# First router of a two-layer block: codes by the eight-maximum, positions by two products, weights worked out in the expert loop

## What is computed

```
logits = where(old_to_new == -1, -inf, x @ gate.T)      # 128 experts, 48 kept
probs  = softmax(logits); top_v, top_i = top_k(probs, 8)
top_v  = top_v / sum(top_v)
flat_e = old_to_new[top_i].reshape(-1)                  # in order of token, then rank
pos    = number of earlier entries of flat_e that are the same expert
valid  = pos < 96                                       # capacity
xb[flat_e, pos] = x[token]                              # kept ones only
out    = (silu(xb @ gate_e) * (xb @ up_e)) @ down_e     # per expert, 96 rows
final[token] += out[flat_e, pos] * top_v * valid
```

## Time and profile before

| | us |
|---|---|
| median of 3 runs (lowest, highest) | 1669.9 (1666.23, 1676.31) |
| profiled execution, its own time | 1677.43 |
| its span | 1675.6 |
| PE busy | 1406.2 (84%) |
| DVE busy | 1156.0 (69%) |
| ACT busy | 822.9 (49%) |
| POOL busy | 782.8 (47%) |
| routing phase | from about 260 to 338.7 |
| expert phase's loop | from 338.7 to 430.6 |

### The profile page before, as it was taken

One profiled execution on the slowest core, in us unless ns is written; L12 is line 12 of the kernel. 1 busy time (PEld: TensorE's weight loads), 2 busy tenths in 40 slices (PEclk: granted clock), 3 DMA queues, 4 the chain that ended last, 5 costly groups with the idle time before them and its releaser, 6 DMA issues. The chain is left out here.

```text
span 1675.6 us, 38381 instructions
## 1 busy us (share of the span) xinstructions
PE 1406.2 (84%) x14345; PEld 999.1 (60%) x14345; DVE 1156.0 (69%) x2350; ACT 822.9 (49%) x2163; POOL 782.8 (47%) x1118
## 2 busy tenths in 40 slices
PE   5988994189545899999999999999999999976675
PEld 2543342066422567777777677777777777765465
DVE  6887126923475788888888788888887888833623
ACT  3334871043132466665665565665665666632122
POOL 5100000177213366467567467566566566543443
PEclk9999996589877999999999899999999999987788
DMA  8200005066723464565565464654555555331884
GB/s 280 74 2 2 2 1 157 1 199 211 256 58 66 114 148 122 149 177 125 160 156 131 128 160 122 162 153 144 139 157 148 119 160 148 99 107 57 241 253 130
DMA packets 249433, 218.72 MB, mean 131 GB/s; under 512 B 88770, under 2 KB 224962, under 8 KB 247200
## 3 DMA queue, kind: packets, MB, share of 16 engines
q1 hardware_dynamic: 234992, 192.41, 42.7%
q0 software_dynamic: 5712, 15.60, 2.8%
q10 hardware_dynamic: 8544, 8.26, 1.6%
HBM read 133.85 MB, written 82.25 MB: 129 GB/s over the span
## 5 line engine op out<-in xcount | busy, mean ns | idle before, releaser
L1825 DVE SCALAR_TENSOR_TENSOR d_conv<-d_big,all_cw,d_conv 128x1023 f32<-128x1023 f32 (+2 forms) x192 | 245.4, 1278 | 45.6 <-ACT d_conv L2067 43.6
L1547 PE MATMUL d_big<-all_xn_t,all_w 128*128 128x512 f32 x512 | 252.6, 624 | 18.7 <-DVE d_conv L1825 11.9
L1547 PEld LDWEIGHTS d_big<-all_xn_t,all_w 128*128 128x128 f32 x512 | 93.8, 198 | 101.4 <-issue 88.2
L2166 ACT COPY d_ys<-d_big 128x128 f32<-128x128 f32 x256 | 61.0, 266 | 177.7 <-PE d_big L1715 139.8
L2301 POOL TENSOR_TENSOR d_y<-d_y,all_xn 128x256 f32<-128x256 f32 x128 | 96.9, 757 | 107.3 <-DVE d_y L1977 89.5
L1753 PE MATMUL d_big<-all_wo,d_yt 128*128 128x256 f32 x512 | 125.5, 391 | 13.8 <-DVE d_yt L1902 13.8
L2258 POOL TENSOR_TENSOR d_vs<-d_vs,d_sv 128x1024 f32<-128x1024 f32 x32 | 61.2, 1912 | 135.6 <-DMA d_vs<-turned_v_scratch 134.3
L1686 PE MATMUL d_big<-all_w,all_xn_t 128*128 128x256 f32 x512 | 122.6, 383 | 0.0
L1753 PEld LDWEIGHTS d_big<-all_wo,d_yt 128*128 128x128 f32 x512 | 96.9, 197 | 26.3 <-issue 14.4
L1876 DVE SCALAR_TENSOR_TENSOR d_AI<-d_big,d_b_col,d_decay 128x256 f32<-128x256 f32 x256 | 104.3, 474 | 2.0 <-PE d_big L1560 1.2
L1686 PEld LDWEIGHTS d_big<-all_w,all_xn_t 128*128 128x128 f32 x512 | 93.7, 190 | 17.7 <-issue 7.2
(11 more groups left out here) (436 smaller groups left out, 3483.2 us busy)
## 6 DMA issues: line engine op xcount, KB each, us to landing
turned_kq_scratch<-d_turned SPq DMA_DIRECT2D x32, 512.0 KB, 3.8
d_kq_tok<-turned_kq_scratch SPq DMA_DIRECT2D x128, 128.0 KB, 3.1
turned_v_scratch<-d_vs SPq DMA_DIRECT2D x16, 1024.0 KB, 4.1
d_vs<-turned_v_scratch SPq DMA_DIRECT2D x64, 256.0 KB, 5.6
grouped_y_scratch<-d_yx SPq DMA_DIRECT2D x32, 512.0 KB, 3.7
d_yx<-grouped_y_scratch SPq DMA_DIRECT2D x128, 128.0 KB, 3.1
all_w<-in_L_attn_W_qkvz SPq DMA_DIRECT2D x16, 768.0 KB
l_hold<-in_L_ffn_gate_up_proj SPq DMA_DIRECT2D x48, 192.0 KB, 3.5
```

The costliest lines, as they stand in the source:

```text
L1547: mm = pe.matmul(big[0][:, c, :], w_sb[par][:, k, n * DK:(n + 1) * DK], xn_t[:, k, c * 512:(c + 1) * 512], start=(k == 0), stop=(k == KD - 1))
L1825: dve.scalar_tensor_tensor(conv[:, sh:T], src[:, 0:T - sh], cw[:, bass.ds(g, 1), COLUMN_OF[j], 3 - sh], conv[:, sh:T], ALU.mult, ALU.add). ...
```

## The change

The gate and map loads are issued in attention, behind the clearing of the second mixture's slots (`clear_slots`). Logits are shifted four tiles at a time. `chosen` is made by ScalarE. Positions come out of two products: `ahead_t = sum of chosen of earlier tiles with ones + chosen with before`, then times `same`, in fp32. The code of each chosen expert (`fine`) plus its position stands at the expert's place, all else far below it (a code is at least 2^14), and an eight-maximum takes the eight codes, in the order of codes, not of probabilities. Doubles are found by one 8x8 comparison per token. The 128-wide one-hots are 64 compares with a pointer scalar; the rank product moves from POOL to VectorE, the row product from VectorE to ScalarE.

Since codes are no longer in rank order, the weights need the index search and the 64 picks after all; these, a second slot calculation and the matching of slots with weights run on VectorE in the expert loop (`weigh(e)`), and ScalarE's diagonals stand at experts 41, 43, 45 and 47.

```diff
+class Routing:
+    def load(self, sp, gate_t, old_to_new):
+        sp.dma_start(self.gate[:, :, :], gate_t.rearrange("(k p) e -> p k e", p=P)).then_inc(self.loaded, 16)
...
 # router0_phase, TensorE
-            for t in range(TT):
-                pe.wait_ge(chosen_s, t + 1)
-                pe.transpose(tr_ps[:, t, :], chosen[:, t, :], ident_bf[:, :]).then_inc(turned_s, 1)
...
+            def ahead_of(t):
+                pe.wait_ge(chosen_s, t + 1)
+                for b in range(t):
+                    pe.matmul(at_ps[t // 4][:, t % 4, :], chosen[:, b, :], ones[:, :], start=(b == 0), stop=False,
+                              skip_group_check=True)
+                pe.matmul(at_ps[t // 4][:, t % 4, :], chosen[:, t, :], before[:, :], start=(t == 0), stop=True,
+                          skip_group_check=True).then_inc(at_mm, 1)
+            def position(half):
+                pe.wait_ge(at_c, half + 1)
+                for t in range(4 * half, 4 * half + 4):
+                    pe.matmul(ps_ps[half][:, t % 4, :], ahead_t[:, t, :], same[:, :], start=True, stop=True,
+                              skip_group_check=True).then_inc(pos_mm, 1)
...
+            for t in range(6):
+                ahead_of(t)
+            position(0)
+            for t in range(6, TT):
+                ahead_of(t)
+            position(1)
 # ScalarE
+            def choose(t):
+                act.wait_ge(taken_s, t + 1)
+                act.activation(chosen[:, t, :], taken[:, t, :], ACT.Relu, scale=-1.0).then_inc(chosen_s, 1)
+            def keep_ahead(half):
+                act.wait_ge(at_mm, 4 * half + 4)
+                act.copy(ahead_t[:, 4 * half:4 * half + 4, :], at_ps[half][:, :, :]).then_inc(at_c, 1)
...
+                act.activation(hot_id[:, t, :, 0, :], hot_e[:, t, :, :], ACT.Copy, scale=row_f[:, 0:1]).then_inc(low_s, 1)
 # VectorE
+            def best(t):
+                dve.wait_ge(exp_s, t + 1)
+                dve.max(top[:, t, :], prob[:, t, :]).then_inc(top_s, 1)
+                if t:
+                    keep_code(t - 1)
+                dve.wait_ge(top_s, t + 1)
+                dve.match_replace(taken[:, t, :], top[:, t, :], prob[:, t, :], -1.0).then_inc(taken_s, 1)
+            def sorted_codes(half):
...
+                dve.tensor_tensor(code[:, at, :], ps_ps[half][:, :, :], fine[:, at, :], ALU.add).then_inc(code_s, 1)
+                dve.wait_ge(code_s, half + 1)
+                for t in range(4 * half, 4 * half + 4):
+                    dve.max(top_code[:, t, :], code[:, t, :]).then_inc(top_code_s, 1)
+            shift_logits(0)
+            best(0)
+            best(1)
+            shift_logits(1)
...
-                for r in range(TOPK):
-                    dve.scalar_tensor_tensor(junk[:, t * TOPK + r, :], iota_f[:, :], idx_f[:, t, r:r + 1], packed[:, t, :],
-                                             ALU.is_equal, ALU.mult, accum_out=code[:, t, r:r + 1]).then_inc(code_s, 1)
...
-                dve.tensor_tensor(hot_c[:, t, :, :], iota_b[:, :].unsqueeze(1).broadcast_to([P, TOPK, P]),
-                                  row_b[:, t, :].unsqueeze(2).broadcast_to([P, TOPK, P]), ALU.is_equal).then_inc(hot_s, 1)
+                for r in range(TOPK):
+                    dve.tensor_scalar(hot_c[:, t, r, :], iota_b[:, :], row_v[:, t, r:r + 1], None, ALU.is_equal).then_inc(hot_c_s, 1)
 # experts0_phase, VectorE, after product(e) of each expert
+            def weigh(e):
+                if e < TT:
+                    index_of(e)
+                elif e == TT:
+                    dve.wait_ge(idx_s, TT)
+                    then(dve.tensor_copy(idx_f[:, :, :], top_idx[:, :, :]))
+                elif e <= LAST_CODE:
+                    for k in range(CODES * (e - FIRST_CODE), min(CODES * (e - FIRST_CODE) + CODES, NR)):
+                        code_of(k)
...                                      # LAST_CODE = 30; then split, doubles, place, shares, weights_by_slot: one an expert
 # ScalarE
-                if e % 4 == 0 and e < 2 * TT:
-                    diagonals(e // 4)
+                if e >= EK - TT and e % 2:
+                    diagonals((e - EK + TT) // 2)
```

More of the change, by code:

```diff
@@ L629, in router0_phase @@
+def router0_phase(nc, xn, xn_t, routing, ranks, xn_dram, buffers, gu_t, down_t):
     with ExitStack() as ctx:
@@ L808, in _ @@
-            then(dve.tensor_copy(idx_f[:, :, :], top_idx[:, :, :]))
-            for t in range(TT):
-                dve.wait_ge(count_mm, 4 * (t // 4) + 4)
-                then(dve.tensor_copy(count[:, t, :], ct_ps[t // 4][:, t % 4, :]))
-                if t == 0:
-                    dve.tensor_copy(total[:, 0, :], count[:, 0, :]).then_inc(total_s, 1)
-                else:
-                    dve.wait_ge(total_s, t)
-                    dve.tensor_tensor(total[:, t, :], total[:, t - 1, :], count[:, t, :], ALU.add).then_inc(total_s, 1)
@@ L835, in _ @@
-            n += 2
-            dve.wait_ge(v, n)
-            for r in range(1, TOPK):
-                then(dve.tensor_tensor(equal[:, :, 0:r], new_f[:, :, 0:r], new_f[:, :, r:r + 1].broadcast_to([P, TT, r]),
-                                       ALU.is_equal))
-                then(dve.tensor_reduce(extra[:, :], equal[:, :, 0:r], AX.X, ALU.add))
-                then(dve.tensor_tensor(pos_f[:, :, r], pos_f[:, :, r], extra[:, :], ALU.add))
-            then(dve.tensor_scalar(over[:, :, :], pos_f[:, :, :], float(CAP), float(NONE), ALU.is_ge, ALU.mult))
@@ new lines, in _ @@
+            then(dve.tensor_scalar(drop_row[:, :], map_row[:, :], -1.0, NEG, ALU.is_equal, ALU.mult))
+            dve.tensor_scalar(same[:, :], map_row[:, :], map_col[:, 0:1], None, ALU.is_equal).then_inc(same_s, 1)
+            then(dve.tensor_scalar(map_code[:, :], map_row[:, :], 1.0, float(1 << SHIFT), ALU.add, ALU.mult))
+            shift_logits(0)
+            best(0)
+            best(1)
+            shift_logits(1)
+            for t in range(2, TT):
+                best(t)
+            keep_code(TT - 1)
@@ L846, in _ @@
+            sorted_codes(0)
+            sorted_codes(1)
+            dve.wait_ge(top_code_s, TT)
+            dve.wait_ge(made, 6)
+            slots.split(dve, top_code)
+            slots.doubles(dve)
+            slots.place(dve, slot_f)
             then(dve.tensor_copy(slot_i[:, :, :], slot_f[:, :, :]))
@@ new lines, in shares @@
+            def shares():
+                then(dve.tensor_reduce(wsum[:, :], ranks.top[:, :, :], AX.X, ALU.add))
+                then(dve.reciprocal(wrec[:, :], wsum[:, :]))
+                then(dve.tensor_tensor(share[:, :, :], ranks.top[:, :, :], wrec[:, :].unsqueeze(2).broadcast_to([P, TT, TOPK]),
+                                       ALU.mult))
+                then(dve.tensor_scalar(valid[:, :, :], slots.pos_f[:, :, :], float(CAP), None, ALU.is_lt))
+                then(dve.tensor_scalar(kept_f[:, :, :], slots.new_f[:, :, :], 0.5, None, ALU.is_gt))
+                then(dve.tensor_tensor(valid[:, :, :], valid[:, :, :], kept_f[:, :, :], ALU.mult))
+                then(dve.tensor_tensor(share[:, :, :], share[:, :, :], valid[:, :, :], ALU.mult))
@@ new lines, in weights_by_slot @@
+            def weights_by_slot():
+                wide = [P, TT, TOPK, TOPK]
+                then(dve.tensor_tensor(met[:, :, :, :], ranks.slot[:, :, :].unsqueeze(3).broadcast_to(wide),
+                                       slot_r[:, :, :].unsqueeze(2).broadcast_to(wide), ALU.is_equal))
+                then(dve.tensor_tensor(part[:, :, :, :], met[:, :, :, :], share[:, :, :].unsqueeze(2).broadcast_to(wide), ALU.mult))
+                dve.tensor_reduce(weight[:, :].rearrange("p (t r) -> p t r", r=TOPK), part[:, :, :, :], AX.X, ALU.add
+                                  ).then_inc(weight_s, 1)
@@ new lines, in weigh @@
+            def weigh(e):
[7 more added lines that the diff above has]
+                        code_of(k)
+                elif e == LAST_CODE + 1:
+                    dve.wait_ge(code_s, NR)
+                    slots.split(dve, code)
+                elif e == LAST_CODE + 2:
+                    slots.doubles(dve)
+                elif e == LAST_CODE + 3:
+                    slots.place(dve, slot_r)
+                elif e == LAST_CODE + 4:
+                    shares()
+                elif e == LAST_CODE + 5:
+                    weights_by_slot()
```

291 lines of the change are left out of this document (168 added, 123 removed).

## The result

| | median us | lowest, highest | runs |
|---|---|---|---|
| before | 1672.61 | 1666.23, 1676.31 | 4 |
| after | 1654.97 | 1652.3, 1658.11 | 4 |

A forecast was written before the change was run, and what follows sets the result against it. Router bound by a VectorE chain, expert loop by TensorE, so work moved into VectorE's gaps is free. Terms -4.0 -23.9 -3.7 +3.3 = -28.3 us, giving 1641.6 us on the median, range 1631 to 1653.

The forecast's parts named there:

- Loads, -4.0: Router start: loads issued early in attention let the first logit product start at about 260.0 instead of 263.99; gain 4.0 us.
- First logits to codes: Router, from first shifted logit to sorted codes: new chain, TensorE's from 8 us on, ends at 16.1 us.
- rival 1: Router: longer new chain (bf16 products at 0.29 or ScalarE late), 5 us less gain, 1647; table loads up to 4; chance 0.09.
- Codes to first hot_e: Router: split 0.9, doubles 2.45, place 0.75, integer steps 0.9; 5.0 us, first hot_e at 21.1 instead of 45.0.
- One-hots, -3.7: Router's one-hots: eight compares at 0.125 us each, tile 1.74 instead of 2.18 us; 14.9 against 18.56, gain 3.7.
- Expert loop, +3.3: Expert loop: VectorE's some 28 us of added work mostly fits its gaps; overruns and moved diagonals cost 3.3 us.
- +1.1 for overruns: Expert loop: VectorE's doubles and weights by slot overrun the 1.75 us gap by 0.7 and 0.4 us.
- +1.9 of the last burst: Expert loop's end: diagonals behind silu(47) hold ScalarE, delaying the last tiles' copies and last scatter by 1.9 us.
- rival 2: Expert loop: POOL becomes the bound, its issues lengthened a tenth by VectorE's two-tensor SBUF reads; 8 us, 1650; chance 0.11.
- Rival 3: Expert loop: VectorE's queue becomes the bound, all 28 us exposed; 1670, no change; chance 0.04.
- Rival 4: Expert loop: stalls drop TensorE's clock; low throughout costs 50 us, 1692, slower than before; chance 0.02.
- Rival 5: Router start: early loads not there by 260, change undone by its loads; 1646; chance 0.02.

The follow-up runs named there:

- e3_loads_in_router: After with the gate and map loads moved back from attention's SP queue to the head of the router's; 1661.79 us, ratio 0.9919.
- e4_diagonals_early: e1_iota_psum with ScalarE's four bursts of diagonals at experts 37, 39, 41, 43 instead of 41, 43, 45, 47; 1644.44 us, ratio 0.9794.
- e1_iota_psum: After with the 64 picks reading the row of expert numbers from PSUM instead of SBUF; 1643.03 us, ratio 0.9869.
- e5_broadcast: After with row positions (hot_c) again by one broadcast compare per tile instead of eight small ones; 1655.72 us, ratio 0.9902.

## Why the prediction was wrong

- **Loads, -4.0.** Right: the first product stands at the router's start, and e3_loads_in_router gives the 4.0 us back.
- **First logits to codes.** The direction and the structure were right, the chain 1.6 us shorter than said (14.5 for 16.1). The steps of best tiles are 0.66 apart (0.68 said). The terms that were mis-sized are TensorE's last two: the sums of tiles 6 and 7 took 0.8 us where 1.8 stood in the sum, and the products of position(1) 1.16 where 1.9 stood, since the clock was at 1.00 in 278 to 281, not at the low level on which I had sized them. It is not always so: in e3_loads_in_router, at the lower clock, the sums of tiles 6 and 7 took 1.6 us. Relu stood behind exp with 0.31 us and no table load, so rival 1 fell altogether; the Trainium skill, ScalarE: Activation LUTs, "Table sets: the hidden batching unit", says that relu lies in every set, and the trace agrees.
- **Codes to first hot_e.** 4.84 for 5.0: three doubles steps 0.72 apart, as said.
- **One-hots, -3.7.** The term of 0.125 us a compare is wrong; it is 0.163, inside its bounds. 64 of them are 2.4 us more, and the gain is 1.3. The estimate that the prediction worked out from the Trainium skill's table, a step of about 0.10, is not borne out either.
- **Tail, 0.** Right: 7.37 for 7.38.
- **Expert loop, +3.3: this is the step that failed.** It costed VectorE's new work only by VectorE's gaps before TensorE ("three picks are 0.82: free"). They were: e4_diagonals_early carries all that work in a loop as long as before's, so the +1.1 for overruns and +0.3 for spacing were nothing. The +1.9 of the last burst was real (1.6 us from e1_iota_psum to e4_diagonals_early), but lay behind POOL's backlog in after. What cost the rest is rival 2: it named POOL and the picks' two tensors in SBUF, and had a chance of 0.11. Its "8 us" came on top of the +3.3; measured, POOL's issues took 9.5 us more, and they took the place of the +3.3, as POOL's queue alone then ended the loop. A price per issue was not in my sum, though the earlier trace rows showed how little POOL waited (1.23 us before that scatter; 4.0 us for result tiles in the whole loop, by its grouped lines above), and the earlier trace rows showed one tensor_tensor slowed from 1.21 to 1.68 beside POOL. The Trainium skill, GPSIMD Engine Reference, "Key points", has the rule on two SBUF inputs. The runs bear it out: up to 1.71 us an issue with two, 0.98 with one.
- **Attention, +4.2: not in the sum at all.** Of the change only three loads lie there, and kernels without them were late as well (262.74, and 261.75 with the very attention of before). The profiled execution caught a cast that waited for the end of a second memset, and ScalarE's copy that stands at 49.53 in before stood at 54.98, 5.4 us later. Differences of the clock in the rest of attention left 4.2 of it. It is in part a matter of how the two engines are shifted against each other: the casts took 1.38 at most in before and in e5_broadcast, 3.01 or more in the other kernels with long memsets. Why one kernel falls on another shift than the next stays open, and so does how much of the 4.2 us the median holds, as each kernel has one trace.
- **The other rivals.** Rival 3: VectorE's 26 us were hidden. Rival 4: the clock stood at 1.00 in the loop's middle. Rival 5: the loads were there. Of what was to show the forecast, the first transposition (307.6 for 307) came where said, once the 4.2 us of attention are taken off, and first hot_e 2 us earlier (283.0 for 285); the loop, at 99.25 us, was past the 92 to 96; the sign against it, issues over 1.35 us apart, was there too: 1.71 + 0.30.
- **The sum.** With the loop at its measured +8.4 in place of +3.3 the sum is -23.2; attention's 4.2 make it -19.0, and the spans show -19.3. That this comes out within 0.3 us is partly luck, as the other misses (-0.2, -1.7, +2.4, -0.8) cancel. The medians show -17.6.

What stays open: the stretch behind the last scatter, in which no edit changes a line that would matter, took 1237.9 to 1250.3 us in these profiled executions. A kernel's time carries some us of that which are not its edits' (e1_iota_psum's profiled one most of all), and no run here shows why. The -0.8 us between before and after is a sum of larger shifts both ways: one instruction of the second layer (d_S) starts 286.9 us behind the last scatter in before (716.50) and 295.3 in after (706.36), 8.4 us later, and by the end that is gone.

## What to carry to other kernels

Before work is moved into an engine's gaps, list what else shares a path to memory with it: here the receiving gaps were really free, and an engine two steps off the chain paid. Where POOL issues indirect DMAs back to back, count its reserve over the whole stretch, and give VectorE's instructions beside it at most one operand in SBUF. Look for long memsets on POOL beside VectorE's casts: they can hold one for several us. Whether cutting them into pieces helps is not shown here.

## What was unexpected of the hardware

- A group of three picks (0.82 us) with two tensors in SBUF lengthened the indirect DMA's issue beside it from 0.97 to as much as 1.66 to 1.71 us: nearly the whole group. Ten of after's 17 long issues were of that length, the other seven 1.26 to 1.40. With one operand in PSUM it was 0.98.
- VectorE's fp32 to bf16 cast of 128x1024 took 0.69 us with no memset beside it (at 47.24 in after), and up to 6.45 beside memsets of POOL of 3.51 us each. Beside a memset it ended 0.54 to 0.56 us after that or the next memset's end, whatever their length.
- Eight 128-wide bf16 compares with a pointer scalar (1.30 us) were slower than one broadcast compare of 1024 (1.22, the next instruction 1.13 after its start).
